# The scatter of an earlier group's rows, moved on GpSimd from ahead of the attention to behind the keys' sum inside it

## The chip, the cores and the metric

The kernel runs on one core of one Trainium2 chip. Its metric is the device time of one execution in microseconds. The core has five engines that run at the same time and meet only through semaphores: TensorE (PE in the profile, its weight loads PEld), VectorE (DVE), ScalarE (ACT), GpSimd (POOL) and SyncE (SP), which only issues transfers here. Each engine works through its own instructions strictly in order, so an instruction that waits holds up everything behind it on its engine.

## The reference, cut to what matters

One decoder layer over 32 sequences of 128 tokens with 128 features. Three parts follow one another, each added to its input and normalised:

```python
x = layernorm(x + mamba(x))            # W_in, causal convolution, selective scan over 16 states, W_out
x = layernorm(x + attention(x, ctx))   # 16 heads of 8, rotary positions, causal mask, Wo, bo
x = layernorm(x + experts(x))          # 8 experts, the top 2 of each token
```

In the experts' part each token has two gates, and its row goes through two of the eight experts (`silu(x @ w1.T) * (x @ w3.T) @ w2.T`).

## The kernel before, in words

The 32 sequences are worked on in G = 8 groups of four (S = 4, so 512 tokens in a group). For each group m there are two stages, one after the other:

- **the scan of m**: 16 states, n = 0 to 15. ScalarE makes the decay (L588), GpSimd the input `du * b` (`times_b`, L420), VectorE runs the recurrence (L861), TensorE adds the results up (L1339).
- **the attention of m**: TensorE multiplies with W_out (`first_out`, L1379), which signals `o_ps` once for each half (two sequences) of the group. VectorE takes the statistics (`first_stats`, L899) and normalises (`first_norm`, L914). TensorE transposes the result (`x1_t`, L1396), ScalarE copies it out (`x1_in`, L613), the queries follow (L1402), and then four rounds t = 0 to 3, one for each sequence: scores (L1417, L1424), maxima on VectorE (L930), exponentials on ScalarE (L623), transposes of the probabilities (L1433), their copies (L631 on ScalarE, L945 on VectorE) and the product with the values (L1457).

Work of other groups is woven in. With w = m - 1, e = m + 1 and c = m + 2, the attention of m also holds the keys of e and the first three `times_b` of e, and the scan of m holds the convolution of c and the router of w. Each engine has this order written out by hand.

The router gives each token of a group two positions in a table in DRAM, `xg`. `scatter(w)` writes the group's rows there: 8 indirect DMAs on GpSimd (4 sequences x 2 gates), each of 128 rows with 130 floats, from `x2_all` at the places in `pos`. It waits for `pos_sb` and `row_sb`. What waits for the scatter is `spots_out` of the next routed group on VectorE (L1022, it writes `pos` again), `b_low` on GpSimd for a group three further back, and, at the very end, SyncE before the experts' rows are loaded.

On GpSimd the attention of m holds, in order: `masks(m)` (L440, L443), `scatter(m - 2)` from m = 2 on (L461), `add_bo(m)` (L454, waits for all of the normalised x1), `step_size(e)` (L404, L406, L409, waits for `q_sb`), `add_k(e)` (L449, the keys' sum, waits for VectorE's L889), and `times_b(e, 0..2)` (L420), which waits until TensorE has all scores of m. After the last group `scatter(6)` and `scatter(7)` follow. Then come the experts: a loop over 72 tiles of 128 rows.

`keep_warm` (L1387) is a row of matmuls whose result nobody uses, between W_out and the transposes of x1.

Of the kernel before, what the change touches and what calls it, by code (L numbers as in the profile page):

```python
# [15 lines left out]
G = B // S  # L16
# [23 lines left out]
def build(nc, a, out):  # L40
    ctx = ExitStack()
    with ctx:
# [232 lines left out]
        def at(eng, name, count):  # L275
            if count > 0:
                eng.wait_ge(s[name], count)

        def parts(m):

            return (m - 1 if m else None), (m + 1 if m + 1 < G else None), (m + 2 if m + 2 < G else None)
# [84 lines left out]
        def _(pool):  # L366
# [34 lines left out]
            def step_size(m):  # L401
                at(pool, "softp", m + 1)
                at(pool, "a_ps", 2 * NST * m)
                g_.tensor_tensor(delta[:, :, :], zpos[:, :, :], zabs[:, :, :], ALU.add).then_inc(s["delta_sb"], 1)  # L404
                at(pool, "delta_sb", m + 1)
                g_.tensor_tensor(du[:, :, :], delta[:, :, :], u[:, m % 2], ALU.mult).then_inc(s["du_sb"], 1)  # L406
                at(pool, "du_sb", m + 1)
                for h in range(2):
                    last = g_.memset(delta[:, h, :].rearrange("p (s t) -> p s t", s=S)[:, :, 0:1], RESET)  # L409
                last.then_inc(s["delta_set"], 1)  # L410

            def times_b(m, n):
                at(pool, "du_sb", m + 1)
                at(pool, "b_sb", NST * m + n + 1)
                if n < 3:
                    at(pool, "s_ps", 16 * m)
                    at(pool, "h_sb", 2 * NST * m)
                else:
                    at(pool, "h_sb", 2 * (NST * m + n - 3) + 2)
                g_.tensor_tensor(bu[:, n % 3], du[:, :, :], b_row[:, n % 3, :].unsqueeze(1).broadcast_to((P, 2, T)), ALU.mult).then_inc(s["bu_sb"], 1)  # L420

            def times_c(m, n):
                at(pool, "h_sb", 2 * (NST * m + n) + 2)
                at(pool, "c_row_sb", pooled_done(m, n))
                before = POOLED.index(n) - 1
                at(pool, "y_sum", 17 * m + (POOLED[before] + 1 if before >= 0 else 0))
                g_.tensor_tensor(hc_pool[:, :, :], hst[:, n % 3], c_row[:, :].unsqueeze(1).broadcast_to((P, 2, T)), ALU.mult).then_inc(s["hc_pool_sb"], 1)  # L427

            def b_low(m, n):
                at(pool, "bc_mid_s", m + 1)  # L430
                if m:
                    at(pool, "hc_pool_sb", pooled_done(m - 1, 6))
                at(pool, "bu_sb", NST * (m - 1) + n)
                at(pool, "scat", (m - 3) * 2 * S * 16)
                g_.tensor_tensor(bc3[64:96, m % 2, :], bc_rest[64:96, :], bc_mid[64:96, :], ALU.subtract).then_inc(s["bc3_low"], 1)
                at(pool, "bc3_low", m + 1)

            def masks(g):
                at(pool, "mask_load", 16 * g + 16)
                g_.tensor_scalar(pad[:, :], mask_b[:, :], 0.0, NEG, ALU.is_equal, ALU.mult).then_inc(s["pad_sb"], 1)  # L440
                at(pool, "pad_sb", g + 1)
                at(pool, "s_ps", 16 * g)
                g_.tensor_tensor(mbias[:, :, :], pad[:, :].rearrange("p (s t) -> p s t", s=S),  # L443
                                 causal[:, :].unsqueeze(1).broadcast_to((P, S, L)), ALU.add).then_inc(s["mask_sb"], 1)

            def add_k(g):
                at(pool, "rotk_sb", 2 * g + 2)
                at(pool, "k_heads_sb", 4 * g)
                g_.tensor_tensor(qk[:, 1, :], rotk[:, 0, :], rotk[:, 1, :], ALU.add).then_inc(s["k_sb"], 1)  # L449

            def add_bo(g):
                at(pool, "x1_sb", S * g + S)
                at(pool, "wo_ps", 2 * g)
                g_.tensor_tensor(x1b[:, :, :], x1[:, :, :], bo_b[:, :].unsqueeze(1).broadcast_to((P, S, D)), ALU.add).then_inc(s["x1b_sb"], 1)  # L454

            def scatter(w):
                at(pool, "pos_sb", w + 1)
                at(pool, "row_sb", w + 1)
                for t in range(S):
                    for k in range(2):  # L460
                        pool.indirect_dma_start(xg[:, :], bass.IndirectOffsetOnAxis(ap=pos[:, t, k:k + 1], axis=0),  # L461
                                                x2_all[:, w * S + t, :], None).then_inc(s["scat"], 16)
# [4 lines left out]
            for m in range(G):  # L467
                w, e, c = parts(m)
                for n in range(NST):
                    if n in POOLED and n != 12:  # L470
                        times_c(m, n)
                    if n + 3 < NST:
                        times_b(m, n + 3)
                    if n == 12:
                        times_c(m, n)
                    if n == 6 and e is not None:
                        b_low(e, 10)
                if m == 0:
                    at(pool, "w_later", 16 * NL)
                    add_k(0)  # L480
                masks(m)
                if m >= 2:
                    scatter(m - 2)
                add_bo(m)
                if e is not None:
                    at(pool, "q_sb", 2 * m + 1)
                    step_size(e)
                    add_k(e)
                    for n in range(3):
                        times_b(e, n)  # L490
            scatter(G - 2)
            scatter(G - 1)

# [1210 lines left out]
```

## Time and profile before

| | |
|---|---|
| median of 3 runs | 1165.22 us (1157.1, 1165.22, 1165.36) |
| the profiled execution | 1163.2 us, of which its span (first to last instruction) is 1161.4 us |
| TensorE's mean granted clock | 0.962 of full |
| busy share of the span | PE 88%, DVE 69%, ACT 65%, POOL 52% |
| the chain that ended last | PE 62%, ACT 14%, DVE 10%, issue 7%, POOL 4%, DMA 2% |

The busy share says how long an engine had something in execution; the chain says which work each stretch of time was waiting for.

### The profile page before, as it was taken

To read this page: it belongs to the slowest core of one execution; us is meant where nothing else is said; L and a number is where in the kernel's file an instruction comes from. 1 tells how busy PE (TensorE), PEld (TensorE's weight loads), DVE (VectorE), ACT (ScalarE), POOL (GpSimd) and SP (SyncE) were. 2 spreads that over 40 slices of the span, in tenths; PEclk is the share of its full clock that TensorE was granted. 3 is DMA by queue.
4 is the path that set the end of the run, shared out by engine and by line. 5 is a ranking of instruction groups with operands and counts; after the bars stand their busy time and mean duration, and the time that the engine had idled before them with its cause. 6 is when DMAs were issued, how large, how long until landed. Compare 5 with 4: busy or idle time off the path is not lost.

```text
span 1161.4 us, 19208 instructions
## 1 busy us (share of the span) xinstructions
PE 1022.0 (88%) x5287; PEld 562.4 (48%) x5288; DVE 804.3 (69%) x1625; ACT 759.5 (65%) x2101; POOL 600.3 (52%) x388
## 2 busy tenths in 40 slices
PE   6799889989988988988899887977945999999987
PEld 2344544544454454445445534532533666666662
DVE  1597798788679868867986796798653544444437
ACT  2778877967786777679676775964742444444446
POOL 2595277278627936872794487379132333322210
PEclk9899999999899999999998999998987999999999
DMA  4000000000100000010000000000422111111134
GB/s 113 6 5 24 6 1 10 19 1 1 39 9 1 18 29 2 0 37 11 1 16 22 1 1 29 1 1 9 154 101 56 42 41 41 41 43 44 41 100 145
DMA packets 39402, 36.56 MB, mean 31 GB/s; under 512 B 6561, under 2 KB 35361, under 8 KB 38945
## 3 DMA queue, kind: packets, MB, share of 16 engines
q1 hardware_dynamic: 33792, 25.99, 7.7%
q0 software_dynamic: 4352, 8.99, 2.2%
q10 hardware_dynamic: 1184, 0.70, 0.3%
q8 instruction: 34, 0.56, 0.2%
q14 instruction: 40, 0.32, 0.1%
HBM read 23.99 MB, written 11.67 MB: 31 GB/s over the span
## 4 chain that ended last, share of the span: by engine, by line
PE 62%; ACT 14%; DVE 10%; issue 7%; POOL 4%; DMA 2%; SPq 1%; another core or an unknown queue 0%; DVEq 0%; POOLq 0%; ACTq 0%
PE y_ps L1339 13%; ACT prob L623 8%; PE bank L1616 6%; PE bank L1630 6%; PE bank L1617 6%; PE bank L1261 5%; DVE scan L861 4%; PE bank L1424 3%; PE y_ps L1622 3%; POOL hc_pool L427 2%; PE bank L1433 2%; PE bank L1457 2%; PE bank L1315 2%; PE bank L1326 1%; PE bank L1360 1%
## 5 line engine op out<-in xcount | busy, mean ns | idle before, releaser
L420 POOL TENSOR_TENSOR scan<-du,w 128x1024 f32<-128x1024 f32 x128 | 298.8, 2358 | 153.0 <-PE y_ps L1424 88.1
L861 DVE TENSOR_TENSOR_SCAN scan<-bank,scan 128x512 f32<-128x512 f32 x240 | 282.1, 1209 | 22.1 <-ACT bank L588 20.6
L588 ACT ACTIVATE bank<-delta,a_neg 128x512 f32<-128x512 f32 x240 | 163.5, 691 | 54.0 <-DVE scan L861 52.6
L1339 PE MATMUL y_ps<-w,ident 128*128 128x512 f32 x352 | 166.9, 596 | 0.0
L498 POOL DMA_INDIRECT y<-aoT,dest x72 | 69.2, 962 | 172.9 <-DVE aoT L1193 166.2
L868 DVE TENSOR_TENSOR w<-scan,bank 128x1024 f32<-128x1024 f32 x88 | 106.1, 1206 | 16.4 <-DVE scan L861 6.8
L571 ACT ACTIVATE w<-bank 128x512 f32<-128x512 f32 x121 | 71.3, 589 | 69.1 <-PE bank L1315 67.1
L1152 DVE TENSOR_TENSOR zpos<-zabs,bank 128x512 f32<-128x512 f32 x74 | 50.8, 687 | 78.8 <-PE bank L1617 77.7
L1339 PEld LDWEIGHTS y_ps<-w,ident 128*128 128x128 f32 x352 | 68.0, 193 | 62.0 <-issue 57.3
L623 ACT ACTIVATE prob<-y_ps,nmax 128x128 f32<-128x128 f32 x256 | 91.2, 430 | 0.4 <-DVE nmax L930 0.4
L623 ACT ACTIVATE prob<-bank,nmax 128x128 f32<-128x128 f32 x256 | 89.8, 387 | 2.2 <-DVE nmax L930 2.2
L461 POOL DMA_INDIRECT xg<-x_all,pos x64 | 62.5, 976 | 54.7 <-DVE pos L1022 36.7
L427 POOL TENSOR_TENSOR hc_pool<-scan,c_row 128x1024 f32<-128x1024 f32 x32 | 76.5, 2390 | 26.5 <-DVE scan L861 22.7
L1616 PE MATMUL bank<-w,qk 128*128 x148 | 76.8, 601 | 0.5 <-ACT qk L771 0.5
L1617 PE MATMUL bank<-w,qk 128*128 x148 | 76.1, 596 | 0.0
L1630 PE MATMUL bank<-prob,delta 128*128 x576 | 76.1, 275 | 0.0
L788 ACT ACTIVATE delta<-y_ps 128x512 f32<-128x512 f32 x72 | 43.0, 597 | 50.3 <-PE y_ps L1622 49.6
L1433 PE MATMUL bank<-ident,prob 128*128 128x128 f32 x512 | 69.4, 278 | 5.5 <-ACT pT L631 5.2
L775 ACT ACTIVATE zabs<-bank 128x512 f32<-128x512 f32 x74 | 44.2, 597 | 44.5 <-PE bank L1616 44.5
L1339 PE MATMUL y_ps<-hc_pool,ident 128*128 128x512 f32 x128 | 64.2, 626 | 8.9 <-POOL hc_pool L427 8.8
L1433 PEld LDWEIGHTS bank<-ident,prob 128*128 128x128 f32 x512 | 55.4, 141 | 33.4 <-issue 20.4
L1630 PEld LDWEIGHTS bank<-prob,delta 128*128 128x128 f32 x576 | 70.0, 192 | 0.0
(257 smaller groups left out, 2057.4 us busy)
## 6 DMA issues: line engine op xcount, KB each, us to landing
qk<-xg SPq DMA_DIRECT2D x79, 65.0 KB, 1.9
cn<-in_ctx SPq DMA_DIRECT2D x8, 256.0 KB, 2.9
mask_b<-in_mask SPq DMA_DIRECT2D x8, 256.0 KB
w<-in_w1T SPq DMA_DIRECT2D x1, 2048.0 KB, 8.8
w<-in_w3T SPq DMA_DIRECT2D x1, 2048.0 KB, 7.7
prob<-in_w2T SPq DMA_DIRECT2D x1, 2048.0 KB
u<-y SPq DMA_DIRECT2D x4, 512.0 KB, 5.9
w<-in_x SPq DMA_DIRECT2D x6, 256.0 KB, 3.0
```

Source lines behind the costliest of these rows:

```text
L420: g_.tensor_tensor(bu[:, n % 3], du[:, :, :], b_row[:, n % 3, :].unsqueeze(1).broadcast_to((P, 2, T)), ALU.mult).then_inc(s["bu_sb"], 1)
L427: g_.tensor_tensor(hc_pool[:, :, :], hst[:, n % 3], c_row[:, :].unsqueeze(1).broadcast_to((P, 2, T)), ALU.mult).then_inc(s["hc_pool_sb"], 1)
L571: A(b_row[:, n % 3, :], bank[1 if n < 3 else 0], ACT.Copy).then_inc(s["b_sb"], 1)
L588: A(bank[(6 if n else 4) + h], delta[:, h, :], ACT.Exp, scale=a_neg[:, h, n:n + 1]).then_inc(s["a_ps"], 1)
L623: last = A(prob[:, t % 2, c, j, :], bank[2 + c][:, j * L:(j + 1) * L], ACT.Exp, bias=nmax[:, t % 2, h:h + 1], accum_out=den[:, t % 2, h:h ...
L861: v_.tensor_tensor_scan(hst[:, n % 3, h, :], bank[(6 if n else 4) + h], bu[:, n % 3, h, :], 0.0, ALU.mult, ALU.add).then_inc(s["h_sb"], 1)
L868: TT(hc[:, i % 3], hst[:, n % 3], bank[2].unsqueeze(1).broadcast_to((P, 2, T)), ALU.mult).then_inc(s["hc_sb"], 1)
L1339: last = MM(y_ps[:, h], ident[:, :], hc_pool[:, h, :] if n in POOLED else hc[:, ON_DVE.index(n) % 3, h, :], start=False, stop=False, skip_ ...
L1433: last = TR(bank[6 + c % 2][:, j * L:(j + 1) * L], prob[:, t % 2, c, j, :], ident[:, :])
L1616: MM(bank[b], xsT[:, b, :], w1[:, bass.ds(e, 1), :].rearrange("p a f -> p (a f)"), start=True, stop=True).then_inc(s["up_ps"], 1)
L1617: MM(bank[2 + b], xsT[:, b, :], w3[:, bass.ds(e, 1), :].rearrange("p a f -> p (a f)"), start=True, stop=True).then_inc(s["up_ps"], 1)
L1630: last = MM(bank[6][:, b * P:(b + 1) * P], gT[:, b, c, :], w2[:, bass.ds(e, 1), c, :].rearrange("p a d -> p (a d)"), start=(c == 0), stop= ...
```

## The change

The eight indirect DMAs of `scatter(m - 2)` leave their place between `masks(m)` and `add_bo(m)` and stand between `add_k(e)` and `times_b(e, 0)`. The last group has no e, so the scatter that it carried, `scatter(5)`, now stands behind `add_bo(7)`, ahead of `scatter(6)`. No instruction is added or dropped, and no other engine's order changes.

```diff
                 masks(m)
-                if m >= 2:
-                    scatter(m - 2)
                 add_bo(m)
                 if e is not None:
                     at(pool, "q_sb", 2 * m + 1)
                     step_size(e)
                     add_k(e)
+                    if m >= 2:
+                        scatter(m - 2)
                     for n in range(3):
                         times_b(e, n)
+            scatter(G - 3)
             scatter(G - 2)
             scatter(G - 1)
```

## Rows read from the trace of the kernel before

**Rows 1.** The page: busy time, share of the span, instructions of each engine.
```profile
PE 1022.0 (88%) x5287; PEld 562.4 (48%) x5288; DVE 804.3 (69%) x1625; ACT 759.5 (65%) x2101; POOL 600.3 (52%) x388
```
**Rows 2.** Windows, GpSimd's masks to times_b, groups 1 to 6: stretch, length, busy, clock, DMA.
```profile
192.84:232.07 39.23, 38.28 (x238) 21.54 (x239) 30.86 (x76) 35.97 (x136) 10.62 (x8) 1.00 0.08 21
291.27:337.28 46.01, 43.12 (x238) 23.28 (x239) 31.13 (x76) 36.39 (x136) 18.45 (x16) 0.89 0.09 30
397.38:440.46 43.08, 40.06 (x238) 22.26 (x239) 30.91 (x76) 36.29 (x136) 18.37 (x16) 0.96 0.11 32
499.65:542.71 43.06, 40.06 (x238) 22.15 (x239) 30.91 (x76) 36.28 (x136) 18.38 (x16) 0.96 0.10 32
601.91:647.93 46.02, 43.12 (x238) 23.26 (x239) 31.10 (x76) 36.38 (x136) 18.36 (x17) 0.89 0.08 24
706.27:748.81 42.54, 40.19 (x238) 22.06 (x239) 29.77 (x75) 29.83 (x128) 18.37 (x16) 0.96 0.06 20
```
**Rows 3.** Timeline of POOL, scatter(0) in group 2: start, length, idle before, releaser.
```profile
294.73 1.17 POOL L461 DMA_INDIRECT xg<-x_all,pos  x1 [0.18 <-issue]
...
303.79 0.96 POOL L461 DMA_INDIRECT xg<-x_all,pos  x1 [0.31 <-issue]
```
**Rows 4.** The chain that ended last, group 2's first attention steps: start, length, what.
```profile
301.84 1.33 another core or an unknown queue
...
304.64 1.61 PE bank L1396 x2
```
**Rows 5.** Timeline of PE and ACT, group 2: x1's transposes and the copy behind them.
```profile
304.64 0.44 PE L1396 MATMUL bank<-ident,x 128*128 128x128 f32 x2 [0.94 <-DVE x L914]
306.27 0.38 ACT L613 ACTIVATE aoT<-bank 128x256 f32<-128x256 f32 x1 [1.12 <-PE bank L1396]
```
**Rows 6.** Timeline of DVE, statistics of both halves: group 1, then group 6.
```profile
202.62 0.50 DVE L899 BATCH_NORM_STATS2 stats<-bank 128x6 f32<-128x128 f32 x2 [1.08 <-PE bank L1379]
...
203.32 0.46 DVE L899 BATCH_NORM_STATS2 stats<-bank 128x6 f32<-128x128 f32 x2
...
718.21 0.49 DVE L899 BATCH_NORM_STATS2 stats<-bank 128x6 f32<-128x128 f32 x2 [1.54 <-PE bank L1379]
...
720.34 0.49 DVE L899 BATCH_NORM_STATS2 stats<-bank 128x6 f32<-128x128 f32 x2 [1.36 <-remote]
```
**Rows 7.** Windows: group 2 behind x1; x1b to times_b in groups 6 and 1.
```profile
308.00:317.00 9.00, 9.00 (x21) 3.25 (x21) 4.31 (x15) 5.51 (x26) 4.83 (x4) 0.50 0.00 1
...
722.53:748.81 26.28, 25.63 (x178) 13.31 (x179) 20.57 (x54) 23.84 (x117) 7.41 (x6) 1.00 0.00 1
205.84:232.07 26.23, 25.64 (x178) 13.31 (x179) 20.59 (x55) 23.79 (x117) 7.42 (x6) 1.00 0.04 11
```
**Rows 8.** Timelines of POOL and DVE, group 1's attention and the scan behind it.
```profile
218.21 1.30 POOL L449 TENSOR_TENSOR qk<-w 128x512 f32<-128x512 f32 x1 [5.13 <-DVE w L889]
232.07 6.99 POOL L420 TENSOR_TENSOR scan<-du,w 128x1024 f32<-128x1024 f32 x3 [12.57 <-PE y_ps L1424]
...
237.68 1.23 DVE L861 TENSOR_TENSOR_SCAN scan<-y_ps,scan 128x512 f32<-128x512 f32 x1 [0.27 <-ACT y_ps L588]
...
242.13 0.17 DVE L1022 CAST pos<-posf 128x8 int32<-128x8 f32 x1
```
**Rows 9.** Timelines of ACT, PE and DVE, group 1, rounds 2 and 3.
```profile
223.13 0.60 ACT L631 ACTIVATE pT<-bank 128x512 f32<-128x512 f32 x1 [0.40 <-PE bank L1433]
229.91 0.60 ACT L631 ACTIVATE pT<-bank 128x512 f32<-128x512 f32 x1
...
230.85 0.68 DVE L945 COPY pT<-bank 128x512 f32<-128x512 f32 x1
```
**Rows 10.** Timelines of PE, POOL and DVE, the last group's ranks beside scatter(6).
```profile
863.15 0.35 PE L1490 MATMUL bank<-oh_all,ones_b 128*128 128x8 bf16 x8
863.76 0.95 POOL L461 DMA_INDIRECT xg<-x_all,pos  x1 [0.30 <-issue]
866.31 0.19 DVE L1006 TENSOR_TENSOR rank<-bank,base 128x32 f32<-128x32 f32 x1 [3.69 <-remote]
```

## The prediction

> **What bounds the kernel now.** I first read the page's busy shares: GpSimd works 52% of the span and TensorE 88% [rows 1], so moving ten microseconds of GpSimd's time is worth nothing as busy time. It can count only through who waits. The groups run one after the other, scan then attention, so what a stage loses the whole kernel loses. The second view is therefore a table by stage. From GpSimd's masks to its first times_b is the attention up to the point where all scores are done, and every group has the same instructions in it, apart from the scatter that begins with group 2 and some work that group 6 lacks. Group 1, without a scatter, takes 39.23 us. Groups 2 to 5, with it, take 46.01, 43.08, 43.06 and 46.02 us at nearly equal instruction counts (238 matmuls in each), and their granted clock is 0.89 to 0.96, where group 1 has 1.00 [rows 2]. That is the reader's first sight of it: 3.8 to 6.8 us per group are lost beside the scatter, and part of it is TensorE's clock.
>
> Where it goes is shown by the chain of waits and the timelines of group 2. The eight DMAs are issued from 294.73 to 303.79 us, each 0.96 us long, plus a gap of 0.30 [rows 3]. In that stretch VectorE waits 1.33 us for something that the profile cannot name, between the two halves of the statistics [rows 4]. What it waits for by the program is `o_ps`, a signal of TensorE. In group 1 the second half's statistics follow with no wait at all; in group 6 there is the same wait of 1.36 us, and the first half is 0.46 late as well (1.54 against 1.08) [rows 6]. Next, TensorE's transposes of x1 last 0.44 us from 304.64, yet ScalarE's copy of them starts only at 306.27, after 1.12 us of idle time [rows 5]. So **signals that TensorE gives come late** while the later half of a scatter is in flight, up to 11.5 us after its first DMA (306.27 - 294.73) and 2.5 us after its last. The last group shows it again: the rank matmuls end at 863.5, scatter(6)'s last DMA is issued at 863.76, and VectorE goes on at 866.31, 2.8 us late and 2.55 after that DMA [rows 10]. I do not know the mechanism; the trace gives the place and the price.
>
> The gaps have a second cost. TensorE stands idle 0.94 us and again after 305.1 [rows 5], and from 308 to 317 us it runs at a granted clock of 0.50, the lower level of 1.2 GHz, wholly busy [rows 7]. Nine microseconds there hold 4.5 us of work at 2.4 GHz.
>
> **The change part by part.**
>
> *Taken from the front of the attention: the scatter of groups 2 to 5.* I take group 1 as the pattern, as it has the same steps: 46.01 - 39.23 = 6.78, 43.08 - 39.23 = 3.85, 43.06 - 39.23 = 3.83 and 46.02 - 39.23 = 6.79, together 21.25 us. Of group 2's 6.78, the two late signals are 1.33 + 1.12 = 2.45 and the low clock is the other 4.3, which fits the 4.5 above.
>
> *Group 6* has less work for ScalarE and cannot be held against group 1 as a whole. But from its x1b to its times_b it takes 26.28 against 26.23 [rows 7], so its loss lies ahead of that: the late halves, 0.46 + 1.36 = 1.82 us [rows 6]. *Group 7* I put at nothing. The sum of what goes is 21.25 + 1.82 = 23.07 us.
>
> *Added inside the attention: GpSimd's own time.* With group 1's times, add_k ends at 219.51 and times_b starts at 232.07, released by TensorE's last scores [rows 8]. The eight DMAs take 9.06 + 0.96 = 10.0 us [rows 3], so they end near 229.7: 2.3 us to spare, at no cost. Were this cover gone, one more lies behind it: the first times_b is done 2.3 us after its start, at 234.4, and VectorE's first scan step starts at 237.68, held by ScalarE and not by GpSimd [rows 8], so 3.3 us more are free. Who waits behind the moved DMAs on GpSimd is only times_b. VectorE's L1022 needs the scatter to have landed; it comes at 242.13 [rows 8], some 10 us after the landing at about 232. add_bo and step_size come no later than in group 1. SyncE's queue passes nothing.
>
> *Added inside the attention: late signals of TensorE.* Before, this part had no scatter beside it, so no row shows the cost, and I bound it. From below: nothing, if each late signal meets slack. No gain is possible, since nothing there becomes shorter. From above: 2.45 us a group, the loss in group 2's front, or 6.78 with the clock's fall. The late signals would lie 7.1 to 11.5 us after the first DMA (301.84 and 306.27 against 294.73), that is from 226.8 to 231.2 in group 1's times. There ScalarE works through the exponentials nearly without a gap, and its one direct wait for TensorE in it is the copy at 229.91, which follows on with no idle time; the copy a round earlier waited 0.40 [rows 9]. So one tight signal instead of three. One late signal costs 1.12 to 1.36; with luck part of it meets slack. I take 1.0 us a group, nearer to one such row than to all of them, over groups 2 to 6: 5.0 us. TensorE has other rounds' work queued there, so I take its clock as full.
>
> *scatter(5), now behind add_bo(7),* has its late half beside rounds 0 and 1 of the last attention, where less other work covers it. Bounds: 0 to 2.8, the late ranks [rows 10]. I take 1.5 us.
>
> **A rule against the change.** The moved DMAs stand beside VectorE's copies. One of those, 512 wide, lasts 0.68 us and reads a PSUM bank [rows 9], and beside the scan's end each DMA kept its 0.96 us [rows 3]. The Trainium skill (SBUF — State Buffer, section "SBUF: two separate sides") says that GpSimd can't write descriptors while VectorE runs a mode that takes both port pairs, as a float32 copy from SBUF to SBUF does. These copies come from PSUM, so I read the rule as not meeting them; if it did, the scatter would run past 229.7, which is the rival "stretched" below.
>
> **The sum.** 23.07 - 5.0 - 1.5 = 16.6 us. Against the profiled execution, 1163.2 us, that is 1146.6; its span is 1161.4 and the 1.8 around it stay. The median of the three runs, 1165.22, is 2.0 above it and would give 1148.6, while one run had 1157.1. I predict 1148 us.
>
> **The rivals.**
>
> *The same loss in the new place (the gain half eaten).* Each scatter costs 2.45 inside the attention, as in group 2's front. For it: the cause moves with the DMAs, and every round needs several signals of TensorE. Against: only one is tight. 6 x 2.45 = 14.7, so 23.07 - 14.7 = 8.4 us gained: 1155 to 1157.
>
> *The scatter is not what delays the signals.* Groups 0 and 1 differ from the others in being first, too. Then the front stays as it is and nothing changes: 1163 to 1166. For it: the loop over the experts issues a similar DMA per tile without such an unnamed wait; against it: the same wait in five groups and the ranks, each ending with the scatter. The Trainium skill (SBUF — State Buffer, "Who interferes with whom") says a DMA never contends with a compute engine and TensorE waits for nobody; the late signals beside the DMAs speak against using that here. By that rule the time would be this rival's.
>
> *Slower: TensorE's clock falls inside the attention.* If late signals leave TensorE idle among the rounds and its clock goes to 1.2 GHz for 9 us as in group 2 [rows 7], each of six groups pays 2.45 + 4.5 = 7.0 us: 42 against 23.07, so 19 us slower, 1182. It decides from 3.85 us per scatter on (23.07 / 6). Against it: TensorE is wholly occupied in group 1's rounds, 38.28 of 39.23 us [rows 2].
>
> *Stretched.* If each DMA also waited out one VectorE copy of 0.68, the scatter would end 8 x 0.68 = 5.4 later, of which 2.3 + 3.3 = 5.6 are covered: no change to the sum. It joins the forecast.
>
> **How the numbers follow.** Forecast (1140 to 1152) 0.56; same loss in the new place (1152 to 1159) 0.22; no effect (1160 to 1166) 0.13; slower 0.09. The lower end is 1163.2 - 23.07 = 1140. The upper end takes in the second case and part of the third, 1162. About 1% is what a measurement of this kernel can tell from no change; 1% under 1165.2 is 1153.6. Faster by more: the forecast and a little of the second case, 0.61. Within: 0.30. Slower: 0.09.
>
> **What would show it.** In the new profile masks to times_b should last 39.2 to 42 us in groups 2 to 5 at a clock of 1.00; the wait of L899 for the unnamed releaser should be gone, and ScalarE's L613 should follow the transposes at once; ScalarE's copies L631 should wait about 1 us once per attention; GpSimd's times_b should still be released by TensorE. I am wrong if the unnamed wait stays, if the clock falls in the rounds, or if the rounds lose more than 2 us.

## The result, and the profile after

The changed kernel takes **1191.2 us** (median of 4 runs, 1188.47 to 1196.13), the kernel before 1161.52 us (4 runs, 1157.1 to 1165.36). The ratio is 1.026, with a 95% interval of 1.020 to 1.032: slower, outside the range of 1140 to 1162. The record gives no chip number for these runs; since the traces of both kernels show late signals and no later trace does, I take them as one chip, or one chip's condition at that time. The experiments fell on five chips (7, 3, 11, 12 and 5). The changed kernel ran on two of them (3 and 5), and on neither is it slower than the kernel before. Both facts need an explanation, and the first is read from the trace.

The profiled execution took 1189.66 us with a span of 1187.9. The page's busy line answers to [rows 1]; the line of the chain shows the news.

```profile
PE 1025.5 (86%) x5287; PEld 565.9 (48%) x5288; DVE 804.7 (68%) x1625; ACT 758.1 (64%) x2101; POOL 600.4 (51%) x388
...
PE 56%; ACT 17%; DVE 11%; issue 7%; another core or an unknown queue 4%; POOL 3%; DMA 1%; SPq 1%; DVEq 0%; POOLq 0%; ACTq 0%
```

Nobody has more work (PE 1022.0 before, 1025.5 now), but 4% of the chain, some 48 us, waits for "another core or an unknown queue"; before it was 0%. The table by stage says where (masks to times_b, groups 2 to 6; columns as in [rows 2]):

```profile
289.85:334.70 44.85, 39.68 (x238) 22.15 (x239) 30.96 (x76) 35.98 (x136) 18.47 (x17) 0.96 0.10 31
395.58:444.98 49.40, 41.58 (x238) 23.15 (x239) 30.94 (x76) 35.97 (x136) 18.38 (x16) 0.90 0.09 28
504.17:553.91 49.74, 41.85 (x238) 23.43 (x239) 30.95 (x76) 35.98 (x136) 18.38 (x17) 0.90 0.10 28
614.02:663.44 49.42, 41.59 (x238) 23.17 (x239) 30.95 (x76) 35.97 (x136) 18.40 (x17) 0.90 0.07 22
720.86:772.32 51.46, 43.59 (x238) 23.99 (x239) 29.82 (x75) 29.66 (x128) 18.39 (x17) 0.83 0.06 16
```

They sum to 244.87 us against 220.71 in [rows 2]: 24.2 of the 26.5 us by which the span grew. (Lines behind the edit are one higher than before: L631 is now L632, L945 L946, L1433 L1434.)

Group 3 shows what happens. First GpSimd's timeline (start, length, line, idle before it, releaser): eight DMAs, 1.26 us apart, and then still 12.68 us of waiting for TensorE. In [rows 8] it was 12.57 with no DMA ahead of it, so what holds times_b back is TensorE and not the time that GpSimd spends.

```profile
422.41 1.06 POOL L461 DMA_INDIRECT xg<-x_all,pos  x1 [0.17 <-issue]
...
431.35 0.95 POOL L461 DMA_INDIRECT xg<-x_all,pos  x1 [0.30 <-issue]
444.98 2.35 POOL L420 TENSOR_TENSOR scan<-du,w 128x1024 f32<-128x1024 f32 x1 [12.68 <-PE y_ps L1425]
```

TensorE's timeline:

```profile
425.18 1.09 PE L1434 MATMUL bank<-ident,prob 128*128 128x128 f32 x8
...
426.63 1.13 PE L1425 MATMUL y_ps<-scan,qk 32*128 32x512 f32 x4
434.61 1.94 PE L1434 MATMUL bank<-ident,prob 128*128 128x128 f32 x8 [6.85 <-ACT pT L632]
...
437.85 2.08 PE L1425 MATMUL bank<-scan,qk 32*128 32x512 f32 x4
```

VectorE's, and under it ScalarE's:

```profile
424.00 1.29 DVE L931 TENSOR_REDUCE nmax<-bank 128x4 f32<-128x512 f32 x2 [0.63 <-PE bank L1425]
...
432.50 0.29 DVE L956 TENSOR_TENSOR aoT<-bank,rdenT 128x128 f32<-128x128 f32 x1 [6.22 <-remote]
433.92 0.69 DVE L946 COPY pT<-bank 128x512 f32<-128x512 f32 x1 [1.13 <-remote]
```

```profile
433.87 0.60 ACT L632 ACTIVATE pT<-bank 128x512 f32<-128x512 f32 x1 [8.40 <-remote]
```

VectorE still gets a signal of TensorE promptly at 424.00. TensorE does the product with the values from 424.16 and the transposes from 425.18, all done by 426.3. By the program L956 waits for the first and L632 for both. They go on at 432.50 and 433.87, after 6.22 and 8.40 us of idle time. In a trace without this wait (e7, below) the same two have 0 and 0.39 us, so they are 6.2 and 8.0 us late. The last DMA is issued at 431.35, so the releases come 1.2 and 2.5 us behind it. TensorE, in its turn, can't start the next transposes until ScalarE's copy is done. The same three waits of 6.2, 8.4 and 1.1 us stand in groups 3, 4, 5 and 6; group 2 has 3.42, 5.59 and 2.54. The stretches of four microseconds through it (last columns: granted clock, DMA share, GB/s):

```profile
424.00:428.00 4.00, 3.76 (x47) 2.17 (x47) 2.03 (x5) 1.47 (x9) 3.08 (x4) 1.00 0.20 67
428.00:432.00 4.00, 0.00 (x0) 0.00 (x0) 0.00 (x0) 0.00 (x0) 3.08 (x4) 0.99 0.16 50
432.00:436.00 4.00, 1.39 (x7) 1.42 (x8) 2.33 (x7) 2.13 (x11) 0.30 (x1) 0.50 0.07 21
436.00:440.00 4.00, 3.67 (x10) 1.04 (x8) 0.96 (x3) 4.00 (x24) 0.00 (x0) 0.50 0.00 0
```

For four microseconds three engines do nothing at all while GpSimd issues DMAs. When they come back TensorE has 0.50 of its clock, 1.2 of 2.4 GHz: eight transposes take 1.94 us in place of 1.09, four score products 2.08 in place of 1.13. So a group loses in two ways, a **hold** and a **half-speed stretch** behind it.

The last group shows that it is not TensorE's signals alone. Here the scatter stands behind add_bo(7), and its last DMA is issued at 853.05. VectorE's L936 waits by the program for `p_sb`, which ScalarE gives when a round's exponentials are done, and TensorE's L1418 waits for the same signal. ScalarE's last piece of that work, VectorE's L936 and TensorE's L1418:

```profile
852.17 0.29 ACT L624 ACTIVATION_READ_ACCUMULATOR prob<-y_ps,nmax 128x1 f32 x1
```

```profile
854.13 0.25 DVE L936 RECIPROCAL rden<-den 128x16 f32<-128x16 f32 x1 [1.64 <-remote]
```

```profile
854.16 0.39 PE L1418 MATMUL y_ps<-mbias,identb 128*128 128x512 bf16 x1 [1.75 <-remote]
```

ScalarE is done at 852.46, and in e7 L936 follows without idle time; here both waiting engines go on about 1.7 us later. The ends of TensorE's matmuls are modelled in this profile, so in group 3 the work itself might have been late; in the last group it is the signal.

What was hoped for is there as well: in the front, x1b starts 13.00 us behind masks (408.58 - 395.58), as in group 1 of [rows 2], and VectorE's second statistics follow the first with no wait.

### The profile page after: what moved, and what is told of

The parts are those of the page before. It is cut to its first block, busy times and chain, and to the rows that moved or that the text cites. A ratio compares the mean times of both kernels' runs of the same rounds, so it can differ in the third digit from the quotient of the medians.

```text
span 1187.9 us, 19208 instructions
## 1 busy us (share of the span) xinstructions
PE 1025.5 (86%) x5287; PEld 565.9 (48%) x5288; DVE 804.7 (68%) x1625; ACT 758.1 (64%) x2101; POOL 600.4 (51%) x388
## 4 chain that ended last, share of the span: by engine, by line
PE 56%; ACT 17%; DVE 11%; issue 7%; another core or an unknown queue 4%; POOL 3%; DMA 1%; SPq 1%; DVEq 0%; POOLq 0%; ACTq 0%
PE y_ps L1340 13%; ACT prob L624 9%; PE bank L1617 6%; PE bank L1618 5%; PE bank L1631 5%; PE bank L1262 4%; DVE scan L862 4%; PE bank L1425 3%; PE y_ps L1623 3%; POOL hc_pool L427 2%; PE bank L1458 2%; PE bank L1434 2%; PE bank L1316 1%; PE bank L1281 1%
## 5 line engine op out<-in xcount | busy, mean ns | idle before, releaser
L1434 PE MATMUL bank<-ident,prob 128*128 128x128 f32 x512 | 75.3, 293 | 37.5 <-ACT pT L632 32.7
L1434 PEld LDWEIGHTS bank<-ident,prob 128*128 128x128 f32 x512 | 60.1, 149 | 67.1 <-issue 53.8
```

The lines of the kernel that those rows point to most:

```text
L1434: last = TR(bank[6 + c % 2][:, j * L:(j + 1) * L], prob[:, t % 2, c, j, :], ident[:, :])
```

## The experiments

Each set has its own chip, so each is told with the time that the unchanged kernel had in that set. In the third, fourth and fifth set every time is a single run, as are those of e1, e4, e5, e6 and e8.

**First set (unchanged kernel: 1135.9 us).** Four kernels, all made from the kernel before. `e1_deferred` keeps the slots of all groups and scatters behind the loop:

```
-        pos = sb("pos", [P, S, 2], I32)
+        pos = sb("pos", [P, G, S, 2], I32)
...
-                if m >= 2:
-                    scatter(m - 2)
...
+            for w in range(G):
+                scatter(w)
```

> No scatter runs inside any attention: the slots of all groups are kept, and all eight scatters stand behind the loop, so the end gets some 60 us of scatters that stood elsewhere; only the windows from masks to times_b are compared. Theory A (the back-to-back indirect transfers of GpSimd hold back TensorE's signals to the other engines, and TensorE's clock then falls): groups 2 to 5 take 39 to 40 us each, as group 1 does (39.23), against 44.9 to 49.7 in the changed kernel, at a granted clock of 1.00, and no wait of L632's kind lasts over 3 us. Theory B (the stall comes from another load that grows with the groups, such as the scan's transfers or VectorE's ranks): the windows stay at 43 us or more without any scatter.

`e4_direct_pool` adds to it eight ordinary DMAs of the same tiles, in the changed kernel's place:

```
                     add_k(e)
+                    if m >= 2:
...
+                        for i in range(8):
+                            pool.dma_start(scr[i * P:(i + 1) * P, :], x2_all[:, (m - 2) * S + i // 2, :])...
```

> The kernel with the scatters behind the loop, and in the place where the changed kernel scatters, GpSimd sends the same eight tiles of 128 rows of 130 words to a scratch tensor in DRAM by ordinary transfers; these rows are written for the experiment alone. Theory A1 (it is the indirect form, whose addresses GpSimd writes while it runs): windows of groups 3 to 5 stay at 39 to 41 us and L632's wait under 3 us. Theory A2 (any transfer that GpSimd issues holds the signals): the windows are 45 to 50 us with waits of 5 to 8 us on TensorE, as in the changed kernel. Theory C (GpSimd's time): the windows grow only by what GpSimd spends beyond 12 us before times_b, so hardly at all.

`e5_direct_sp` has the same eight DMAs in SyncE's queue, behind `at(sp, "k_sb", g + 2)`.

> As the run before, but the same eight transfers to scratch are issued by SyncE at about the same time, behind the keys' sum. Theory A1 and A2 (what GpSimd issues): no wait on TensorE over 3 us, windows of groups 3 to 5 at 39 to 41 us. Theory D (the 0.5 MB of traffic itself holds signals, whoever issues it): windows of 45 to 50 us with the same waits of 5 to 8 us.

Group 3 (for e5 too) in the windows of e1, e4 and e5:

```profile
390.35:429.58 39.23, 38.29 (x238) 21.55 (x239) 30.85 (x76) 35.97 (x136) 10.63 (x9) 1.00 0.07 21
```

```profile
388.30:427.55 39.25, 38.29 (x238) 21.55 (x239) 30.87 (x76) 36.01 (x136) 14.86 (x16) 1.00 0.11 35
```

```profile
388.51:427.75 39.24, 38.28 (x238) 21.54 (x239) 30.86 (x76) 36.02 (x136) 10.61 (x9) 1.00 0.13 35
```

All three are at 39.23 to 39.25, the whole at 1161.86, 1163.58 and 1162.26 us (the scatters now stand behind the loop, with nothing beside them). Taken alone, this reads as a clean proof that only the scatter's own DMAs hold signals. It is none: the control is missing. The unchanged kernel took 1135.9 us in this set, some 26 less than in the runs of the result, and the next set shows why that matters.

`e2_spread` puts the eight DMAs one by one between the steps of the attention:

```
                 masks(m)
-                if m >= 2:
-                    scatter(m - 2)
...
+                    scatter_part(m - 2, 0, 1)
+                    at(pool, "yg_sb", 2 * m + 1)
+                    scatter_part(m - 2, 1, 2)
+                    at(pool, "x1_sb", S * m + S)
+                    scatter_part(m - 2, 2, 3)
                 add_bo(m)
...
+                    for j in range(3):
+                        at(pool, "p_sb", 16 * m + (8, 10, 12)[j])
+                        scatter_part(m - 2, 5 + j, 6 + j)
```

> The same eight transfers of each scatter stand one by one between the steps of the attention (behind masks, behind o, behind x1, behind step_size, behind the keys' sum, and three behind parts of the softmax), with 2 to 5 us between them. Theory A, in the form that a signal is held for as long as transfers are queued: each holds a signal for one transfer at most (1.3 us), some hit nothing, so the windows of groups 2 to 5 are 39 to 43 us at a clock of 1.00, and the whole is 1135 to 1155 us. Theory C (what counts is the 10 us that GpSimd spends before times_b): GpSimd spends the same, so the windows stay at 45 to 50 us and the whole at 1180 to 1195 us.

Measured: 1137.74 us, ratio to the unchanged kernel 1.002 (1.001 to 1.0029). Its windows of groups 2 to 5 are 39.83 us. On this chip theory C is out: GpSimd spends the same time on the scatter ahead of times_b and nothing stretches. In the runs of the result it is out by the changed kernel's own trace, where times_b waits 12.68 us for TensorE. The 0.6 us that each group loses fit the third DMA standing ahead of x1b, which starts at 402.29, 14.17 us behind masks in place of 13.0:

```profile
401.32 0.96 POOL L461 DMA_INDIRECT xg<-x_all,pos  x1 [4.12 <-DVE x L936]
402.29 1.29 POOL L454 TENSOR_TENSOR x1b<-x,bo_b 128x512 f32<-128x512 f32 x1
```

**Second set (unchanged kernel: 1135.5 us, 19 runs).** The controls (`e6_before_again`, `e7_after_again`), and two tests of how many DMAs it takes and how far apart.

> The kernel before, unchanged, for a profile of the same chip as the runs beside it. In the first set of experiments the unchanged kernel took 1135.9 us, against 1157 to 1165 us in the runs that the prediction was made from, so the chips differ. If the hold of TensorE's signals is what differs between them, its windows of groups 2 to 5 show less than the 43.1 to 46.0 us of [rows 2] wherever the whole takes 1136 us; if the chips differ elsewhere, the windows stay at 43 to 46 and the difference lies outside them.

> The changed kernel, unchanged. Theory A (the place of the eight transfers decides): it is slower than the kernel before on this chip too, with waits of 5 us or more at L632 in each group from 3 on. Rival (the hold belongs to the one chip of the first result): it comes out within 1% of the kernel before or under it, with windows of 39 to 42 us.

The unchanged kernel, profiled (1135.75 us). Windows of groups 1 to 6:

```profile
190.83:230.05 39.22, 38.28 (x238) 21.56 (x239) 30.83 (x76) 35.95 (x136) 10.60 (x8) 1.00 0.07 21
289.25:328.47 39.22, 38.28 (x238) 21.55 (x239) 30.83 (x76) 35.96 (x136) 18.50 (x16) 1.00 0.11 35
387.67:426.90 39.23, 38.29 (x238) 21.56 (x239) 30.85 (x76) 35.96 (x136) 18.38 (x17) 1.00 0.11 35
487.01:526.24 39.23, 38.29 (x238) 21.57 (x239) 30.85 (x76) 35.97 (x136) 18.39 (x17) 1.00 0.12 35
585.43:624.66 39.23, 38.28 (x238) 21.56 (x239) 30.85 (x76) 35.96 (x136) 18.39 (x17) 1.00 0.09 28
682.97:723.89 40.92, 39.98 (x238) 22.02 (x239) 29.71 (x75) 29.65 (x128) 18.37 (x16) 0.96 0.06 21
```

This is the kernel of [rows 2], with its scatter in the old place, and it loses nothing beside it: 39.22 us with it and without it. The changed kernel took 1135.47 us, ratio 0.9994 (0.998 to 1.0008); its group 3:

```profile
388.72:427.97 39.25, 38.29 (x238) 21.55 (x239) 30.86 (x76) 36.01 (x136) 18.39 (x16) 1.00 0.12 35
```

and TensorE and VectorE at the place of the hold, 32.1 and 30.8 us into that window, without a wait:

```profile
420.84 1.09 PE L1434 MATMUL bank<-ident,prob 128*128 128x128 f32 x8
```

```profile
419.47 0.29 DVE L956 TENSOR_TENSOR aoT<-bank,rdenT 128x128 f32<-128x128 f32 x1
```

So **on this chip neither place of the scatter costs anything**, and theory A's first half has its evidence in the runs of the result alone. In the same stage the two traces of the unchanged kernel differ in one more thing. The DMA view of the unchanged kernel in group 2 gives the time from issue to landing here, and none in the first trace, for SyncE's loads as for the scatter; the records of the landings are partly missing there. That is no mark of the late signals: the first trace lacks them beside group 1's attention too, which loses nothing, and the changed kernel's page has a landing time of 3.2 us for mask_b. First the trace that the prediction rests on, then this one:

```profile
issues: line engine op xcount, KB each, median us to landing
mask_b<-in_mask SPq DMA_DIRECT2D x1, 256.0 KB
xn<-in_x SPq DMA_DIRECT2D x1, 256.0 KB
xg<-x_all,pos POOLq DMA_INDIRECT x8
```

```profile
mask_b<-in_mask SPq DMA_DIRECT2D x1, 256.0 KB, 3.2
xn<-in_x SPq DMA_DIRECT2D x1, 256.0 KB, 3.0
xg<-x_all,pos POOLq DMA_INDIRECT x8, 2.5
```

Four DMAs in each place (`e3_halves`: `scatter_part(m - 2, 0, 4)` behind masks, `scatter_part(m - 2, 4, 8)` behind add_k):

> Four of the eight transfers stay in the old place behind masks and four go behind the keys' sum. If a hold needs a queue of many transfers (theory A with a backlog), four in a row build up little: windows of 39.5 to 42.5 us, the whole at or 5 to 15 us under the kernel before. If every transfer behind the keys' sum holds a signal, whatever stands before it: the hold is half of the 8.4 us, and the windows are 44 to 47 us.

1136.25 us, ratio 1.0004 (0.9993 to 1.0015), windows 39.23. Equal, and no test of a queue's length, as nothing holds here.

`e8_gap` stretches the scatter in its new place:

```
                         pool.indirect_dma_start(...)
...
+                            for r in range(2):
+                                g_.memset(fill[:, :], 0.0)...
...
```

> The changed kernel with about 1 us of GpSimd's memsets behind each of the eight transfers, which are then some 2.2 us apart in place of 1.26; the scatter lasts 18 us and times_b comes late by about 6 us for this alone, so windows of 45 to 47 us. Theory A with a backlog (transfers come faster than they are worked off, and the signals wait behind the queue): VectorE's and ScalarE's waits on TensorE in the softmax stay under 3 us and the clock stays at 1.00. Rival (the eight transfers hold signals as long as any is under way, however far apart): waits of 8 us or more at L632's kind, and a clock under 0.92.

```profile
420.15 1.06 POOL L464 DMA_INDIRECT xg<-x_all,pos  x1 [0.15 <-issue]
...
435.48 0.97 POOL L464 DMA_INDIRECT xg<-x_all,pos  x1 [0.28 <-POOL fill L468]
436.45 0.94 POOL L468 MEMSET fill<- 128x400 f32 x2
437.47 4.65 POOL L421 TENSOR_TENSOR scan<-du,w 128x1024 f32<-128x1024 f32 x2
```

1152.77 us; windows 44.12 to 44.28 at a clock of 1.00 in groups 2 to 5, a little under the 45 to 47 that I had expected. With no hold on this chip it says nothing of DMAs further apart. This is what the cover is worth: the block from the first DMA on lasts 17.2 us against 9.9 in e7, 7.3 longer, times_b comes 4.9 late (44.14 - 39.25), so 2.4 were free. From one group's masks to the next it is 102.2 us against 98.5 in e7 (495.51 - 393.33; 487.17 - 388.72): 3.7 us of the 4.9 stay, 1.2 are made up behind times_b.

**Third set (unchanged kernel: 1135.0 us).** The hold's second half (`e9_hold`), and three repeats for another chip. In `e9_hold` a chain of 26 memsets of GpSimd makes TensorE wait:

```
             def head_t(g, t, c):
+                if t == 2 and c == 2 and 2 <= g <= 6:
+                    at(pe, "filled", 26 * (g - 1))
```

> No scatter inside any attention (all stand behind the loop), and in groups 2 to 6 TensorE is kept waiting by hand for about 7 us in the place where it stood in the changed kernel (L1434, the third quarter of the third part), by a chain of memsets of GpSimd behind the keys' sum; nothing else is added. If an idle TensorE alone brings the clock down (second half of theory A), the windows of groups 3 to 5 are some 39.2 + 6.9 + 3.3 = 49.4 us at a granted clock near 0.90, and the first work behind the wait runs at 0.50 (L1434 x8 near 1.94 us), on any chip. If the clock fell in the changed kernel for another reason (the transfers' own load), the windows are 39.2 + 6.9 = 46.1 us at 1.00.

A miss of mine: 1164.62 us, windows of 39.48 at a clock of 1.00, because the stall of the changed kernel stands in t = 1. At t = 2 the wait costs TensorE half a microsecond.

```profile
428.68 1.09 PE L1443 MATMUL bank<-ident,prob 128*128 128x128 f32 x8 [0.50 <-POOL fill L461]
```

> The eight transfers one by one through the attention, again. On a chip without the hold: 1137 to 1139 us, windows of 39.8 us. On a chip where the kernel before takes 1157 to 1165 us: theory A (a signal is held for as long as GpSimd's transfers are queued) gives 1140 to 1148 us and windows of 39.8 to 42 us, since at most one transfer is queued at a time; the rival (each of the eight transfers holds signals there, however far apart) gives 1160 us or more.

> No scatter in the attentions, and eight ordinary transfers of GpSimd to scratch in the place of the changed kernel's scatter, again. On a chip without the hold: 1162 to 1165 us and windows of 39.25 us, as the first time. On a chip with it: theory A1 (only transfers whose addresses come from slots hold signals) gives windows of 39 to 41 us; theory A2 (any transfer of GpSimd) gives 45 to 50 us and waits over 5 us at ScalarE's copies.

> Four transfers in the old place and four behind the keys' sum, again. On a chip without the hold: 1134 to 1138 us, windows of 39.23 us. On a chip with it: a hold that needs a long queue gives windows of 39.5 to 42.5 us and 1138 to 1150 us for the whole; a hold by every transfer gives 44 to 47 us.

These three (e10, e11, e12): 1137.2, 1162.59 and 1135.2 us, windows of 39.83, 39.24 and 39.24: a chip without the hold, each as it was on the others.

**Fourth set (unchanged kernel: 1136.0 us).** `e13_hold` has the wait at `t == 1`, with 25 memsets:

> As the first run with a wait made by hand, whose wait stood one part too late and cost TensorE 0.5 us only. Here TensorE waits before the third quarter of the second part, where it stood in the changed kernel, for some 6.9 us in groups 2 to 6; scatters stand behind the loop. If an idle TensorE alone brings the clock down: windows of groups 3 to 5 of 39.2 + 6.9 + 3.3 = 49.4 us at a granted clock near 0.90, L1434 x8 behind the wait at about 1.94 us, on any chip. If not: 39.2 + 6.9 = 46.1 us at 1.00.

```profile
290.31:339.45 49.14, 41.72 (x238) 23.50 (x239) 31.02 (x76) 36.09 (x136) 21.43 (x33) 0.90 0.06 17
399.54:448.69 49.15, 41.73 (x238) 23.51 (x239) 31.03 (x76) 36.10 (x136) 21.43 (x34) 0.90 0.06 17
508.77:557.91 49.14, 41.73 (x238) 23.46 (x239) 31.02 (x76) 36.09 (x136) 21.43 (x33) 0.90 0.06 17
```

```profile
430.58 1.13 PE L1432 MATMUL y_ps<-scan,qk 32*128 32x512 f32 x4
438.49 1.97 PE L1443 MATMUL bank<-ident,prob 128*128 128x128 f32 x8 [6.79 <-POOL fill L461]
```

It reproduces the changed kernel's group 3 (49.40 us, 0.90, 6.85 us of wait, 1.94 us for the transposes) to 0.3 us, on a chip without the hold and with no scatter in the attention. With nearly the same memsets and a wait of only 0.50 us, e9 kept a clock of 1.00. So the half-speed stretch needs neither scatter nor hold, only that TensorE is made idle. It costs 49.14 - 39.23 - 6.8 = 3.1 us, and the whole is 1213.66 us: 51.8 above e1 and 49.0 above e9, each on a chip of its own, for five times 9.9.

> The eight transfers one by one, a third time, for a chip on which the kernel before takes over 1155 us, if this is one: 1140 to 1148 us if a signal is only held while several transfers are queued, 1160 or more if each transfer holds. If the kernel before takes 1135 us here as well, this kernel takes 1137 to 1139 us and tells nothing of the hold but that it is rare among chips.

> The changed kernel with 1 us of memsets behind each transfer, again, for a chip with the hold: windows of 44.1 us at a clock of 1.00, as on the chip without it, if the transfers need to be close together to hold signals; 49 us or more if they hold them at 2.2 us apart too. On a chip without the hold: 1151 to 1154 us, as before.

These two (e14, e15): 1137.04 and 1153.28 us, again a chip without the hold.

**Fifth set (unchanged kernel: 1135.9 us).**

> The changed kernel on one more chip. If the hold is common among chips: 1188 to 1196 us beside 1157 to 1165 for the kernel before. If it belongs to few: 1132 to 1138 us beside 1133 to 1138.

> The eight transfers one by one, for the same chip: 1140 to 1148 us on a chip with the hold, if the transfers hold signals only while several are queued, and 1160 or more if each of them holds; 1137 to 1139 us on a chip without the hold.

> Four and four, for the same chip: on a chip with the hold 1138 to 1150 us if a hold needs a long queue, 1160 or more if not; on a chip without it 1134 to 1138 us.

These three (e16, e17, e18): 1135.57, 1136.85 and 1136.76 us, windows of 39.25, 39.82 and 39.24. So five chips in a row are without a hold: by the unchanged kernel's time on all five, by windows of the changed kernel on 3 and 5, and by the traces of all eighteen experiments, in none of which an engine waits for a releaser that the profile can't name. No version beats both kernels.

## Why the prediction was wrong

**The loss in the front was read rightly, and it belonged to those runs, not to the kernel.** I took 21.25 + 1.82 = 23.07 us from groups 2 to 6. The unchanged kernel without a hold has windows that sum to 197.83 us against 220.71: 22.9. The sum of [rows 2] was right to 0.2 us, group 6's by its late halves too (42.54 - 40.92 = 1.62), and in the new kernel the front has it back. What I could not know from one trace is that the same kernel on five other occasions, each with its own chip, shows none of it.

**"Late signals of TensorE" is the step that failed**, the term of 1.0 us a group "nearer to one such row than to all of them". Measured against the hold-free group it was 5.6, 10.2, 10.5, 10.2 and 10.5 us, the last against the 40.94 of e7: 47.0 in all where I had 5.0. Two readings inside it were wrong. I took the hold as at most 2.5 us, since that was how late the signals of the front came, and counted tight signals by their idle time in group 1. But in the front the first late signal was due at 301.84, only 2.0 us before the last DMA (303.79). In the new place TensorE's work that they wait for is done at 425.2 to 426.3, 2.8 to 3.9 us after the first DMA, and nothing comes until 1.2 to 2.5 us behind the last. In the front the releases (303.19 and 306.27) lie 0.6 ahead of the last DMA and 2.5 behind it. Group 2's in the new kernel (323.96, 325.33 and 326.80, last DMA at 325.73) lie from 1.8 ahead to 1.1 behind. So the late signals come one by one about the end of the burst, much less by when they were given, and in groups 3 to 6 the price is the distance to that end. (In group 2 the hold begins equally early in the burst, but ends 1.8 us ahead of its last DMA, and costs less, 5.6 us.) It is no rule for every signal, though. In the front VectorE got TensorE's signals at 298.43, 299.29 and 301.06, which is 3.7, 4.6 and 6.3 us behind the first DMA, after 1.12, 0.17 and 1.08 us of idle time, exactly what e6 has at the same places. Which signals are held inside a burst stays open. Slack of a microsecond in one signal means nothing against it, for all three engines run dry.

**"I take its clock as full" failed with it.** My rival "slower: TensorE's clock falls inside the attention" is what happened, at 10 us a group in place of 7.0. It named the point from which it decides, 3.85 us per scatter. I held against it that TensorE is busy 38.28 of 39.23 us in group 1; being wholly busy is what makes a stall cost its full length. In e13 6.8 us of waiting and 3.1 of half speed make up 9.9; in the changed kernel's group 3 it is 6.85 and 3.3. The sum of windows, 47.0 - 22.9 = 24.1 us, is nearly the whole growth of the span, 26.5.

**GpSimd's own time** was right: 2.3 us to spare ahead of times_b, measured 2.4 to 2.5 (e8 and the idle time before times_b in e7). Of the further 3.3 behind it only 1.2 showed: what else waits there the runs don't show.

**scatter(5)**: from masks(7) to the last ranks it is 62.6 us before and 63.5 after, so 0.9 net for the 1.5 that I took. Group 7, which I put at nothing, has a loss to the hold in both kernels: without it the same stretch lasts 58.9 and 58.3 us.

**"The scatter is not what delays the signals"** is out for the runs of the result: moving the eight DMAs alone took the late signals out of the front and put them where the DMAs went. On the chip of the second set its outcome came true (a ratio of 0.9994). There the rule of the Trainium skill that I weighed (SBUF — State Buffer, "Who interferes with whom", a DMA never contends with a compute engine) agrees with every window. In the runs of the result it gives no ground for a wait of 8.40 us; that this wait is contention of the kind the rule speaks of isn't shown either.

**What stays open.** Why signals were held in the runs of the result, by what path, which of them, and whether it was that chip or its condition at the time is not settled. That it is tied to GpSimd's DMAs and not to all transfers is only argued, from SyncE's loads, which lie beside group 1's attention without a loss (39.23 us at a DMA share of 0.08). Whether DMAs further apart or four in a row would escape was put to the other chips, and none had the hold to test it on.

## What to carry to other kernels

Before experiments are read, look at the control's trace on the same chip: e1, e4 and e5 each "proved" a cause in windows that the unchanged kernel has too. A wait that a trace can't name, found in one trace, is worth a trace on a second chip before a change is built on it. And where a burst of GpSimd's indirect DMAs does hold signals, price a signal that is due inside the burst as if it came 2.5 us behind the last DMA, the latest seen here, and take that as the upper bound; the lateness seen elsewhere is no bound; on a TensorE that is busy 98% of the stage each microsecond counts in full, with a half-speed stretch behind it.

## What was unexpected of the hardware

- In the runs of the result TensorE's signals to VectorE and ScalarE came up to 8 us late (8.40 us of idle time against 0.39), and one of ScalarE's 1.6 us, beside eight indirect DMAs of GpSimd, 1.26 us apart. On the two other chips where the changed kernel ran (3 and 5) its windows show no loss, and it takes 1135.5 us in place of 1191; the kernel before takes 1135 to 1136 us in all five sets in place of 1161.
- A TensorE idle for 6.8 us in an otherwise full stage comes back at a granted clock of 0.50, and the stage loses 3.1 us more (e13).
- Eight ordinary DMAs of 128 rows of 130 words, from GpSimd or from SyncE, cost the attention nothing on a chip without the hold (39.25 and 39.24 us against 39.23); on GpSimd each takes 0.55 us where an indirect one takes 0.97.
